# Second attention of a gated two-layer decoder block: mask added by VectorE, four-bit weights stored as bf16 halves and turned by DMA, and ternary input steps spread over the groups

## The reference

```python
x = x + tanh(g_xattn[0]) * attn16(LN(x), ctx)            # 16 heads of 32, no mask
x = x + tanh(g_ffn[0])   * bit_ffn(LN(x))                # ternary weights, 8-bit input, conv of 3, silu
x = x + tanh(g_xattn[1]) * attn8(LN(x), ctx, mask)       # 8 heads of 64, masked softmax
x = x + tanh(g_ffn[1])   * fp4_ffn(LN(x))                # w_gate, w_up (1408x512), w_down (512x1408)
# fp4_ffn: inputs, hidden and weights are rounded to four-bit values in blocks of 16 with one scale each
```

## Time and profile before

| what | us |
|---|---|
| three runs | 2139.24, 2143.3, 2150.29 |
| median | 2143.3 |
| the profiled execution | 2140.95 |
| its span in the trace | 2139.2 |
| stages a0, f0, a1, f1 (from the trace) | about 700, 330, 708, 401 |

### The profile page before, as it was taken

The page is one execution under the profiler, slowest core; times in us unless marked ns, Lnnn a source line. Parts: engine busy times, 40 slices in busy tenths (PEclk is TensorE's granted clock), DMA queues, the critical chain, the costliest instruction groups (busy, mean ns, idle before and its releaser), DMA issues. The chain is left out here.

```text
span 2139.2 us, 41319 instructions
## 1 busy us (share of the span) xinstructions
PE 1865.8 (87%) x14714; PEld 1301.2 (61%) x14742; DVE 1417.8 (66%) x2585; ACT 1008.8 (47%) x1311; POOL 1199.1 (56%) x1462
## 2 busy tenths in 40 slices
PE   5799999999997469897598999999999967989995
PEld 3477777777766357786256676676767753444442
DVE  4767777776765467876354666666766456888863
ACT  3167766766768586655223434434434441111110
POOL 3166766766765342434213766766766323777763
PEclk9899999999996679999798999999999988999997
DMA  7445445454430511111542444544444421333222
GB/s 205 110 107 137 117 117 132 114 130 122 113 80 19 184 26 44 34 43 35 179 122 74 137 131 131 150 132 139 146 133 120 158 80 30 67 81 76 70 67 65
DMA packets 238668, 222.43 MB, mean 104 GB/s; under 512 B 116137, under 2 KB 200361, under 8 KB 237993
## 3 DMA queue, kind: packets, MB, share of 16 engines
q1 hardware_dynamic: 238504, 220.22, 37.5%
HBM read 138.61 MB, written 67.53 MB: 96 GB/s over the span
## 5 line engine op out<-in xcount | busy, mean ns | idle before, releaser
L709 POOL TENSOR_TENSOR a_p_hl<-a_p,a_p_hl 125x448 bf16<-125x448 f32 x540 | 564.6, 1047 | 448.0 <-ACT a_p_hl L846 419.2
L836 ACT ACTIVATE a_p<-a_psum 125x1344 f32<-125x1344 f32 x192 | 247.9, 1291 | 135.6 <-PE a_psum L1248 128.5
L1014 DVE TENSOR_REDUCE a_nm<-a_psum 112x1 f32<-112x750 f32 x256 | 237.4, 934 | 98.7 <-PE a_psum L1268 97.6
L846 ACT ACTIVATE a_p_hl<-a_p 125x1344 bf16<-125x1344 f32 x192 | 254.0, 1323 | 82.6 <-PE a_psum L1286 79.1
L1286 PEld LDWEIGHTS a_psum<-a_v_st,a_p_hl 125*128 125x128 bf16 x4608 | 176.7, 98 | 39.6 <-issue 18.5
L1286 PE MATMUL a_psum<-a_v_st,a_p_hl 125*128 125x65 bf16 (+2 forms) x4608 | 188.2, 194 | 10.9 <-POOL a_p_hl L709 4.3
L1158 PE MATMUL a_psum<-a_chl,a_w 128*128 128x375 bf16 x768 | 143.0, 332 | 20.6 <-DVE a_w L905 14.9
L1158 PE MATMUL a_psum<-a_chl,kept_w 128*128 128x375 bf16 x768 | 136.3, 330 | 24.1 <-DVE kept_w L905 17.9
L1268 PE MATMUL a_psum<-a_k_st,a_q_st 96*112 96x375 bf16 x512 | 127.4, 334 | 25.7 <-DVE a_nm L1014 19.1
L1158 PE MATMUL a_psum<-a_w,a_chl 128*125 128x512 bf16 x576 | 140.3, 386 | 9.1 <-DVE a_m_parts L995 5.7
L814 ACT ACTIVATE a_v_st<-a_psum 125x512 bf16<-125x512 f32 x96 | 58.3, 608 | 190.0 <-PE a_psum L1158 190.0
(11 more groups left out here) (251 smaller groups left out, 3851.4 us busy)
## 6 DMA issues: line engine op xcount, KB each, us to landing
a_k<-a_k_tmp SPq DMA_DIRECT2D x64, 375.0 KB, 2.9
a_k_st<-a_k SPq DMA_DIRECT2D x96, 187.5 KB, 3.4
kept_k<-a_k SPq DMA_DIRECT2D x96, 187.5 KB, 3.3
a_c<-in_ctx_t SPq DMA_DIRECT2D x16, 750.0 KB, 6.0
ctx_parts<-a_chl SPq DMA_DIRECT2D x16, 750.0 KB, 9.2
a_chl<-ctx_parts SPq DMA_DIRECT2D x16, 750.0 KB, 6.5
a_q_st<-a_q SPq DMA_DIRECT2D x192, 56.0 KB, 2.2
rounded<-a_fw SPq DMA_DIRECT2D x24, 352.0 KB, 3.7
```

Of the source, the lines that this page charges most:

```text
L709: ins = nc.gpsimd.tensor_tensor(p_hl[0:MC, h % 2, 1, cols], p32[0:MC, h % 2, cols], p_hl[0:MC, h % 2, 0, cols], ALU.subtract)
L836: nc.scalar.activation(p32[0:MC, par, :].rearrange("p (b n) -> p b n", b=3), st[0:MC, :, 0:2 * S], ACT.Exp, scale=scale).then_inc(exp_done, 1)
L846: nc.scalar.activation(p_hl[0:MC, par, 0, :], p32[0:MC, par, :], ACT.Copy).then_inc(phi_done, 1)
L1014: ins = nc.vector.tensor_reduce(out, sm_[0:HALF, 0:2, 0:MK], AX.XY, ALU.max, negate=True)
```

## The change

In a1 the six identity matmuls of `scores_t` go, and DVE adds the mask to the scores in PSUM (`mask_scores`) after slot 4j and before slot 4j+1 and the maximum; ACT's exponentials wait for that. The rounded weights are split into two bf16 parts by DVE (`split_weights`, one quarter later, in `weight_step` at==1) and written as such; SP loads them by transposing DMAs straight into the form that PE uses, three tensors of two parts each. In f1 the weight transposes, their evictions and the loads of w_down go; DVE's turn has another order. In f0 steps are spread over the groups, and `prepare(b+1)` of PE lies between the halves of the down product. The turned mask shares a buffer with the other mask, and is loaded later (`load_turned_masks`). Some buffers shrink.

```diff
@@ a1, SP
+            def load_turned_masks(b):
+                at = b.number
+                sp.wait_ge(mask_ready, at * 2 + 1)
                 sp.dma_start(maskT8[:, :, :], masks[1][bass.ds(at, 1), :, :].rearrange(
                     "o (j p) s -> p (o j) s", j=NJ)).then_inc(maskT_in, 16)
...
+                last = unit[0] == "K" and unit[1][1] == 1 if q == 3 else unit[0] == "Q"
+                if last and 1 <= m <= FP4_PIECES:
+                    sp.wait_ge(f_split, m)
+                    if m + 1 < FP4_PIECES:
+                        load_weight_piece(m + 1)
+                    sp.dma_start(fp4_weights[m - 1][1], fhl[:, :, :]).then_inc(fw_sent, 16)
...
                     sp.wait_ge(fw_sent, FP4_PIECES * 16)
                     sp.wait_ge(unit_mm, units.base + units.k)
-                    for n in range(3):
-                        kept.load(sp, n)
-                if q == 0 and b.number == B - 1 and kept:
+                    kept.load(sp, 2)
+                if q == 1 and b.number == B - 1 and kept:
                     sp.wait_ge(st_ready, B * H)
-                    for n in range(3, 6):
-                        kept.load(sp, n)
+                    kept.load(sp, 0)
+                if q == 0 and b.number == B and kept:
+                    sp.wait_ge(st_ready, B * H + H)
+                    kept.load(sp, 1)
+                if q == 0 and masks and (b + 1).exists():
+                    load_turned_masks(b + 1)
@@ a1, ACT
+                if masks:
+                    act.wait_ge(masked, hd + 1)
+                else:
+                    act.wait_ge(st_ready, H + hd + 1)
@@ a1, DVE
+            def split_weights(m):
+                dve.wait_ge(f_rounded, m + 2)
+                if m >= 1:
+                    dve.wait_ge(fw_sent, m * 16)
+                w = fw[:, m % 2, :]
+                link(nc.vector.tensor_copy(fhl[:, 0, :], w))
+                nc.vector.tensor_tensor(fhl[:, 1, :], w, fhl[:, 0, :], ALU.subtract).then_inc(f_split, 1)
+
+            def mask_scores(b, h):
+                if h == 0:
+                    dve.wait_ge(mask_ready, b.index * 2 + 2)
+                hd = b.index * H + h
+                dve.wait_ge(st_ready, H + hd + 1)
+                scores = st[0:MC, :, 0:2 * S]
+                nc.vector.tensor_tensor(scores, scores, maskT_b[:, b.parity, :, :].rearrange(
+                    "p (k j) s -> p k (j s)", k=3), ALU.add).then_inc(masked, 1)
...
-                    for k in (0, 1):
-                        for unit in slots[4 * j + k]:
-                            unit_step(unit)
+                    for unit in slots[4 * j]:
+                        unit_step(unit)
+                    if masks and b.exists():
+                        mask_scores(b, h)
+                    for unit in slots[4 * j + 1]:
+                        unit_step(unit)
@@ a1, PE
-                    if masks:
-                        nc.tensor.matmul(out, ident_b[0:MC, 0:MC], maskT_b[:, b.parity, j, :], start=True,
-                                         stop=False)
@@ f0, ACT, DVE, PE
-                    if g == 4 and in_range(b + 1):
+                    if g == 6 and in_range(b + 1):
                         scale_input(b + 1)
                         row_factors(b + 1)
-                    if g == 5 and in_range(b + 1):
+                    if g == 7 and in_range(b + 1):
                         round_input(b + 1)
...
-            PREPARE = {0: row_moments, 2: normalise, 3: prepare_factors}
+            PREPARE = {0: row_moments, 2: lambda b: normalise_half(b, 0), 3: lambda b: normalise_half(b, 1),
+                       4: input_maxima, 5: prepare_factors}
...
-                    if g in (3, 5) and in_range(b - 1):
-                        round_hidden(b - 1, 1 - par, 0 if g == 3 else 1)
-                    if g in (5, 7) and in_range(b):
-                        link(row_maxima(b, g - 1))
+                    if g in (6, 7) and in_range(b - 1):
+                        round_hidden(b - 1, 1 - par, g - 6)
+                    if g == 6 and in_range(b):
+                        link(row_maxima(b, 4))
...
-                if in_range(b + 1):
+                if in_range(b + 1) and not in_range(b - 1):
                     prepare(b + 1)
                 if in_range(b - 1):
                     pe.wait_ge(w2_ready, NG)
                     for s in range(2):
+                        if s == 1 and in_range(b + 1):
+                            prepare(b + 1)
@@ KeptTiles
-        sp.dma_start(self.tile(n), rows.rearrange("(c p) n -> p c n", p=P)).then_inc(landed or self.gate_up_in, 16)
+        for part in range(2):
+            sp.dma_start(self.tile(n)[:, part, :, :], self.parts[n][part], transpose=True).then_inc(self.landed[n], 16)
@@ f1, DVE
                 if in_range(t + 3):
                     x_moments(t + 3)
+                if in_range(t):
+                    h_divide(t, par)
+                    h_powers()
                 if in_range(t - 1):
                     h_lo(t - 1, 1 - par)
-                if in_range(t + 2):
-                    x_lo(t + 2)
-                if in_range(t):
-                    h_divide(t, par)
                 for g in range(NG):
-                    if g == 0 and in_range(t):
-                        h_powers()
                     if in_range(t + 1):
                         make_h(t + 1, 1 - par, g)
+                    if g == 0 and in_range(t + 2):
+                        x_lo(t + 2)
@@ f1, PE
-            for n in range(2 * NG):
-                w_transpose(n)
-            pe.wait_ge(wt_done, blocks_before[2 * NG])
+            for n in range(2):
+                pe.wait_ge(kept.landed[n], 32)
             for g in range(NG):
                 gate_up(0, 0, g)
-                w_transpose(2 * NG + g)
-
-            pe.wait_ge(wt_done, blocks_before[NP])
+            pe.wait_ge(kept.landed[2], 32)
```

More of the change, by code:

```diff
@@ L554, in prologue @@
                     if step[0] == "heads":
-                        if step[1] == 0:
+                        if step[1] == 0 and masks:
+                            load_turned_masks(b)
                             load_masks(b + 1)
@@ L819, in unit_hi_part @@
                 elif kind == "M":
-                    if b.number is None or b.number > 0:
-                        act.wait_ge(m_in[k], b.index * 48)
-                    ins = nc.scalar.activation(m_parts[:, k, 0, :], bank[0:H2, 0:S], ACT.Copy)
+                    if not stacked and k == 1:
+                        act.wait_ge(m_in[0], (b.index + 1) * 48)
+                    elif b.number is None or b.number > 0:
+                        act.wait_ge(m_in[k if stacked else 1], b.index * 48)
+                    ins = nc.scalar.activation(m_parts[:, k if stacked else 0, 0, :], bank[0:H2, 0:S], ACT.Copy)
                 else:
@@ L1236, in scores_t @@
                     pe.wait_ge(m_in[h // H2], (b.index + 1) * 48)
-                if masks and h == 0:
-                    pe.wait_ge(mask_ready, b.index * 2 + 2)
                 if not (b.number == 0 and h == 0):
@@ L1243, in scores_t @@
                     out = st[0:MC, j // 2, (j % 2) * S:(j % 2 + 1) * S]
[L1244 to L1246 removed]
                     for t, (at, rows, _) in enumerate(terms):
                         ins = nc.tensor.matmul(out, k_stack(b.parity, at(h), rows)[:, j * MC:(j + 1) * MC],
[L1249 removed]
+                                               q_stack(b.parity, at(h), rows), start=(t == 0),
                                                stop=(t == len(terms) - 1))
@@ L1779, in _ @@
             row_moments(0)
-            normalise(0)
+            for s in range(2):
+                normalise_half(0, s)
             input_maxima(0)
+            input_factors(0)
             def prepare_factors(b):
-                input_maxima(b)
+                input_factors(b)
                 row_factors(b)
@@ L2177, in fp4_ffn @@
         down_ready, y_ready = sem("down_ready"), sem("y_ready")
-        def weight_blocks(n):
-            view = kept.tile(n)
-            f0, m = TR[n % NG]
-            if n < 2 * NG:
-                return [([view[:, f, k * P:(k + 1) * P] for f in range(m)],
-                         lambda part, k=k: gu[:, n // NG, part, k, f0 * P:(f0 + m) * P]) for k in range(KC)]
-            return [([view[:, k, f * P:(f + 1) * P] for k in range(KC)],
-                     lambda part, f=f: wd[:, part, f0 + f, :]) for f in range(m)]
-        NP = 3 * NG
-        blocks_before = [sum(len(weight_blocks(m)) for m in range(n)) for n in range(NP + 1)]
         def turns(engine_loop, turn, enter=None, leave=None):
@@ L2218, in _ @@
             sp.dma_start(g_sb[:, :], gate.partition_broadcast(P)).then_inc(g_in, 16)
-            for g in range(NG):
-                kept.load(sp, 2 * NG + g, down_in[g])
             def turn_input(t, par):
@@ L2538, in gate_up @@
                         for j, (a, b) in enumerate(SPLIT_TERMS):
```

(12 more changed lines are left out.)

166 lines of the change are left out of this document (55 added, 111 removed).

## The result

The changed kernel takes 2163.45 us (median of 4 runs, 2160.01 to 2164.88) against 2141.27 for the one before (4 runs). The ratio on record, estimated from all runs of both, is 1.0089 with a 95% interval of 1.0065 to 1.0113, so about 19 us slower; the two medians alone lie 22 apart. Forecast were 2157 and a range of 2106 to 2182.

The account below looks back on a forecast made before the run. PE was taken to set a1's row, with DVE late once given mask and split. Terms 30+1+8+6-24-7 = +14 on the profiled 2140.95 gave 2155, on the median 2157 us; range 2106 to 2182.

Parts of the forecast that it names:

- The mask's price: a1: one mask addition on DVE takes 1.56 us, from a 125x1344 subtraction; eight a row are 12.5.
- the cost that comes and goes: a1: DVE operations sometimes run far longer beside a busy POOL; 1.3 us a row added for the split's copy.
- The row: a1: a steady row takes 86.5 us, +5.0, with DVE busy 73.5 and idle 13; bounds 76.8 and 91.
- the walk: a1: one row stepped through in queue order, beginning with DVE late; the same instruction comes back after 85.8 us.
- DVE keeps the pace: Rival, a1: PE's stalls stay as now, row 76.8 to 78, total 2099 us; chance 0.13.
- rows and ends: a1: six rows carrying weights cost +30 us, the ends of the weights' stretch +1.
- The mechanism within the row: a1: DVE idles 1.8 us between mask and low part in four of eight heads, 7 a row.
- Last row: a1's last row: longer steps from mask to exponential to next block sum to 38.8 us instead of 30.6, +8.
- Prologue: a1's start: turned mask's load lands about 4 us later, holding ACT's V high part and PE; +6 (3 to 10).
- f0: Ternary stage: spread steps remove PE's wait for DVE's sum, down product waits about 1 a row; -7 (-15 to +5).
- f1: Four-bit feed-forward: earlier start gives -23 us at the first down, turn unchanged at 23.63; together -24 (-32 to -12).
- The loads: Weights' transposing loads land by 1734, before their use at 1760, hidden; rival with slower loads 2180 us, chance 0.1.

Follow-up runs that it names:

- taking 35 of these 47 us away: ScalarE takes slot 4j+1's high part before the exponential instead of behind it, against the changed kernel: 2156.46 us, ratio 1.0042 to the kernel before.
- The later mask: First turned mask made behind head 3's V unit on ScalarE, next row's loaded after head 4, against the changed kernel: 2153.18 us, ratio 1.0028 to the kernel before.
- -14.3 alone: The kernel before with only the changed kernel's ternary stage (f0) put in: 2138.27 us, ratio 0.9943 to the kernel before.
- the old order: VectorE's turn in f1 put back to low part, x low part, division, powers, against the joined kernel: 2112.71 us, ratio 0.9878 to the kernel before.
- the joined kernel: Changed kernel with mask on TensorE, turned mask made later, quarter 3's split behind the K low parts: 2103.53 us, ratio 0.9827 to the kernel before.

## Why the prediction was right or wrong

The direction and the time were right: slower, +19 by the ratio (22 by the medians) against +14. The terms, by the profiled executions:

- **The mask's price**, taken as 1.56 from a row of the same element count, was 1.553. The split was under-sized: its subtraction took 1.24 at the mean against the 0.9 scaled by columns, the copy 0.55, together 1.8 for 1.45 to 1.6. At its shortest the subtraction did take 0.89, but in the median 1.36: the cost that comes and goes, which the forecast looked for in the copy, fell on the subtraction. A third operation of 128x704 grew as well (from 705 to 884 ns, L2105). In all a row had 70 to 72 of DVE work where 73.5 was forecast.
- **The row**, forecast 86.5 by the walk: 86.5 to 87.9 where the clock held, PE 77.1 busy where 75.4 was forecast. "DVE keeps the pace", the rival at 76.8, is refuted, though its sum of 71 in 77 was true: the sum didn't tell that two engines hand one place of scores to and fro.
- **The step that failed** in the rows is "each PE stall in the walk is under 2 us, so I cost the clock at nothing". One stall, ahead of head 7's second scores, is 2.5 to 2.7 in five rows, and behind three of these the next 7 us go at 0.53 to 0.57; the rows of 90.4 and 90.9 are among them, 3 to 5 longer than those where the clock held. The seven rows cost +37.9 for the +31 of rows and ends: the five in the middle +36.1 where 25 stood for them, the first and the last together +1.8 where 6 stood.
- **The mechanism within the row** was half right. I put the row's idle time to the low part that waits behind the exponential, 7 a row; measured are 6.7. But taking 35 of these 47 us away gave 11 over seven rows, and giving the mask to heads without such a unit was as dear as to the others. What TensorE waits for most is the maximum behind the mask, 33.1 us in the seven rows. The experiments show that the head decides: heads 3 and 5, where TensorE has a product between the transposed scores and the next ones, are nearly free, and head 1 costs 16. That this product is the reason isn't shown, since with head 1 the added waits were mostly for a Q's low part and the K stack.
- **Last row** +8: measured +12.9. The walk had steps of 4.3 and 5.8 in turn, two of them 1 longer with the output projection; measured from exponential to exponential are 4.4, 6.4, 9.5, 6.4, 5.5, 5.8 and 5.5. The dearest is one with the output projection, mis-sized by nearly 3. The clock was left out here too: 0.71 in this stretch against 0.90, and one of the projection's two groups of 12 matmuls took 4.41 against 2.80.
- **Prologue** +6: measured +13.5. I let PE's old wait cover a part and put the load about 4 later. In fact SP issued the load 13.5 us after ScalarE's last work ahead of it (1074.9 to 1088.4), and the V units and the maxima stood behind. The later mask gave 8.9 of it back.
- **f0** -7: measured -15.0, and -14.3 alone. The mechanism (a wait of 22 gone, waits of the down product in its place) was right; mis-sized was what the down product's waits cost. The forecast charged 2.8 and 1.1 a row, 27 for seven rows; they rose by 14.8, to 23.0, since 8.2 of waiting was there before. The product's own matmuls took 5.2 more. On the other side the convolution's wait fell by 21.8 and its matmuls ran 12.1 us faster with that stall gone, about the 2.1 for each of six waits that the forecast counted.
- **f1** -24: measured -29.9. The start was near (first down 93.7 after the last exponential for 114.1, -20 where -23 was forecast). "No gain" for the turn failed: -1.1 to -1.3 a turn, by VectorE's order, as the old order showed. I had the new ring at 22.3 to 23.2 and then added 1 of hand-overs; the turn measured 22.3 with them. From the first down to the end the stage is 9.5 shorter, which these turns account for; the 3 of the last turn don't show.
- **The loads** hidden: right. A part of a weight took 5.5 to issue and 7.7 to 9.2 to land, for 6.7 and 11 by block. That rival is out.

The two misses in a1, +7 in the rows and +12.4 in prologue and last row, and those in f0 and f1, -8 and -6, nearly cancel. That the total came within 6 us of the forecast was luck in this; the direction was not, since it rests on the row, which was forecast well.

## What to carry to other kernels

Before moving work from a full engine to one with idle time, ask what stands between the moved operation and the next thing the full engine waits for. TensorE's six matmuls a head cost 17 us here; VectorE's addition, in its idle time by the sum, cost 45. An operation put into an in-order queue delays everything behind it, so its place can be worth more than its length: a mask conversion three units later gave 9 us, and a split two low parts later 16. The same move of the split gave nothing while the mask stood on VectorE, so what a place is worth depends on what else the engine is behind with. And a stall can have a second price: behind some of them the next matmuls go at half speed.

## What wasn't expected of the hardware

- How short a stall can be and still be followed by the lower clock, and that it isn't always: in the changed kernel three of the stalls of 2.65 to 2.68 were followed by 0.53 to 0.57 over 7 us, a fourth by 1.00; in the joined kernel stalls of 1.90 and 1.72 were followed by 0.66 over 5 us, those of 1.00 and 1.32 by 1.00. In the changed kernel the three waits of 1.85 to 1.90 for the K stack were followed by 0.66 once and by 1.00 twice. So the length of the stall alone doesn't tell the cases apart, and what does wasn't tried.
- The first attention with the start of the ternary stage, the same work in all kernels, took 730.8 to 743.4 us from one execution to the next. That alone is 0.6% of the time.
- Transposing loads from device memory weren't slower per block than those from on-chip tiles: 5.5 us of issue for 44 blocks, 3.3 for 22.
